# The first graph attention with joined routing: normalising and masking on ScalarE, rows rated two periods behind

## The reference

```python
h = jnp.einsum('bnf,fd->bnd', x, W)
s_src, s_dst = h @ a[:d], h @ a[d:]
e = s_src[:, :, None] + s_dst[:, None, :]
e = jnp.where(e >= 0, e, NEG_SLOPE * e)
e = jnp.where(A <= 0, -jnp.inf, e)
y = jnp.einsum('bij,bjd->bid', jax.nn.softmax(e, axis=-1), h)
...
logits = xt @ Wr + br
probs = jax.nn.softmax(logits, axis=-1)
top_p, top_idx = jax.lax.top_k(probs, TOP_K)
```

## Time and profile before

| | |
|---|---|
| time, median of 3 runs | 4688.07 us (4686.57 to 4688.72) |
| span of the profiled execution | 4591.2 us |
| what lies around the span (difference to the median) | 96.9 us |
| busy in the span: TensorE, VectorE, ScalarE, GpSimd | 76%, 62%, 46%, 39% |
| the stage in the span: first statistics, last scatter | 2700.1 us, 3049.6 us |
| end of `out(15)`, the last of the attention | 2985.9 us |

### The profile page before, as it was taken

One profiled execution on the slowest core, in us unless ns is written; L12 is line 12 of the kernel. 1 busy time (PEld: TensorE's weight loads), 2 busy tenths in 40 slices (PEclk: granted clock), 3 DMA queues, 4 the chain that ended last, 5 costly groups with the idle time before them and its releaser, 6 DMA issues. The chain is left out here.

```text
span 4591.2 us, 80959 instructions
## 1 busy us (share of the span) xinstructions
PE 3499.2 (76%) x23827; PEld 2132.6 (46%) x23827; DVE 2854.1 (62%) x10855; ACT 2105.7 (46%) x5250; POOL 1802.9 (39%) x2183
## 2 busy tenths in 40 slices
PE   3999995666666638999987867639947788884994
PEld 1333333444444423333345656627736555553663
DVE  5666656555555567777758977832247677763444
ACT  1777773322222216777753236624426555551321
POOL 3555520000000015555456225855545525544444
PEclk8999995555555559999998988869969999996997
DMA  4334318600000014333300012225442000002445
GB/s 130 112 112 118 118 53 368 261 0 0 0 0 0 0 54 126 112 112 111 89 6 2 1 57 71 70 83 153 148 156 80 32 1 20 20 20 85 129 130 162
DMA packets 237349, 378.44 MB, mean 82 GB/s; under 512 B 24832, under 2 KB 157056, under 8 KB 228672
## 3 DMA queue, kind: packets, MB, share of 16 engines
q1 hardware_dynamic: 218688, 337.44, 23.3%
q0 software_dynamic: 18432, 38.31, 2.4%
HBM read 210.70 MB, written 164.95 MB: 82 GB/s over the span
## 5 line engine op out<-in xcount | busy, mean ns | idle before, releaser
L1461 DVE CUSTOM_DVE_ANT_0 mha_seen<-mha_score,mha_mask 128x512 f32<-128x512 f32 x1024 | 684.7, 688 | 378.9 <-PE mha_score L1216 372.9
L1360 ACT ACTIVATE mha_prob<-mha_turned 128x512 f32<-128x512 f32 x1024 | 589.6, 603 | 303.1 <-PE mha_turned L1230 295.9
L1617 PE MATMUL lstm_gates<-lstm_h_part,lstm_w_part 128*128 128x16 f16 x4608 | 277.6, 179 | 327.8 <-DVE lstm_h_part L1832 324.5
L3131 POOL DMA_INDIRECT expert_rows<-expert_y,expert_target x320 | 306.9, 959 | 359.5 <-DVE expert_y L3277 154.6
L1216 PE MATMUL mha_score<-mha_k_rows,mha_q_rows 96*128 96x512 bf16 x1024 | 397.9, 391 | 56.4 <-DMA mha_k_rows<-split_rows 29.5
L1617 PEld LDWEIGHTS lstm_gates<-lstm_h_part,lstm_w_part 128*128 128x128 f16 x4608 | 217.2, 107 | 480.2 <-DVE lstm_h_part L1832 475.5
L1230 PE MATMUL mha_turned<-mha_q_rows,mha_k_rows 99*128 99x512 bf16 x1024 | 389.9, 382 | 8.4 <-ACT mha_turned L1341 6.7
L1564 POOL TENSOR_TENSOR core_mid<-lstm_hist,lstm_per_unit 128x128 f32 x64 | 29.5, 461 | 886.7 <-DVE lstm_hist L1833 886.7
L1704 ACT ACTIVATE lstm_act<-lstm_gates 128x48 f32<-128x48 f32 x512 | 108.0, 211 | 428.6 <-PE lstm_gates L1617 428.6
L1229 PE MATMUL mha_turned<-mha_maskT,core_ident_bf 128*128 128x512 bf16 x768 | 294.8, 384 | 0.3
L3169 PEld LDWEIGHTS expert_out_ps<-expert_w,expert_hid 128*128 128x128 f32 (+1 forms) x2240 | 262.4, 191 | 38.7 <-issue 33.0
(11 more groups left out here) (553 smaller groups left out, 8960.9 us busy)
## 6 DMA issues: line engine op xcount, KB each, us to landing
routed_rows<-lstm_blank SPq DMA_DIRECT2D x66, 1056.0 KB, 27.0
core_params<-adj SPq DMA_DIRECT2D x32, 1024.0 KB, 5.9
gat_adj_raw<-adj SPq DMA_DIRECT2D x32, 1024.0 KB, 5.5
mha_q_rows<-split_rows SPq DMA_DIRECT2D x64, 384.0 KB, 5.3
mha_k_rows<-split_rows SPq DMA_DIRECT2D x64, 384.0 KB, 6.0
expert_x<-routed_rows SPq DMA_DIRECT2D x80, 264.0 KB, 2.8
expert_w<-weights SPq DMA_DIRECT2D x80, 256.0 KB, 3.6
combine_pair<-expert_rows SPq DMA_DIRECT2D x32, 512.0 KB, 4.9
```

The costliest lines, as they stand in the source:

```text
L1360: act.activation(prob[:, n % RING, :], turned[n % 3][:, :], ACT.Exp, scale=-1.0).then_inc(S["prob_ready"], 1)
L1461: dve.tensor_tensor_reduce(seen[n % 2][:, :], score[n % 2][:, :], mask[1 - s][:, t, :], 1.0, 3e38, ALU.add, ALU.min, low[g][:, t, j:j + 1] ...
L1617: return pe.matmul(out, w[:, g * P:(g + 1) * P], h_part[:, part, :], start=False, stop=stop, skip_group_check=True)
L3131: pool.indirect_dma_start(out=core.y_rows[NUMBER][:, :], out_offset=bass.IndirectOffsetOnAxis(ap=target[q][:, t:t + 1], axis=0), in_=y_buf ...
```

## The change

In the first call of `gat_stage`, `normalise` moves from GpSimd to ScalarE (four activations per graph, with scale and shift as operands). `forbid` moves from VectorE to ScalarE, in two halves per graph: relu(1e30 − 1e30·adj), which is 1e30 where there is no edge; VectorE subtracts it in `masked` where it added −1e30. Rows are rated two iterations behind the attention instead of three; TensorE turns rated rows at the end of the iteration before, VectorE marks in even iterations from 4 on and picks in odd ones, behind `out`. GpSimd scatters from iteration 4 on, and the loop runs to B + 3. The logits' `take` stands behind the leaks.

```diff
-        LAST = B + 4 if route else B - 1
+        LAST = B + 3 if route else B - 1
+        MASKS = 2 if route else 1
+        forbidden = m.sb("forbidden", [P, 1]) if route else None
...
             for b in range(LAST + 1):
-                if b + 2 < B:
+                if not route and b + 2 < B:
                     normalise(b + 2)
...
-                if route and b >= 5:
-                    half = (b + 1) % 2 * T
-                    router.scatter(pool, (b - 5) // 2, range(half, half + T))
+                if route and b >= 4:
+                    half = b % 2 * T
+                    router.scatter(pool, (b - 4) // 2, range(half, half + T))
...
+            def normalise(b):
+                need(act, "xt_done", b - 1)
+                for t in range(T):
+                    last = act.activation(xn[b % 2][:, t, :], core.x_res[:, b, t, :], ACT.Identity, bias=shift[:, b, t:t + 1],
+                                          scale=rstd[:, b, t:t + 1])
+                last.then_inc(S["xn_ready"], 1)
+
+            def forbid(b, half):
+                s = b % 2
+                need(act, f"adj_in{s}", 16 * (b // 2 + 1))
+                need(act, "masked", T * (b - 1))
+                act.activation(mask[s][:, 2 * half:2 * half + 2, :], adj_raw[s][:, 2 * half:2 * half + 2, :], ACT.Relu,
+                               bias=forbidden[:, :], scale=-BIG).then_inc(S["mask_ready"], 1)
...
+            if route:
+                need(act, "stat_done", STATS[False])
+                normalise(0)
+                normalise(1)
+                need(act, "const_set", 1)
+                forbid(0, 0)
+                forbid(0, 1)
             rows_in(0)
             project(0)
             for t in range(T):
                 lower(0, t)
             exponent(0, 0)
+            if route:
+                forbid(1, 0)
+                forbid(1, 1)
             rows_in(1)
             project(1)
...
                     exponent(b, 1)
                     take(b, 0)
+                if route and 0 <= b - 2 < B:
+                    router.take_turned(act, b - 2, row_ps)
+                if inside:
                     exponent(b, 2)
                     take(b, 1)
+                if route and b + 2 < B:
+                    normalise(b + 2)
...
-                if route and 0 <= b - 2 < B:
-                    router.take_turned(act, b - 2, row_ps)
                 if inside:
                     take(b, 2)
                 if ahead:
                     lower(b + 1, 2)
-                if route and 4 <= b < B + 4 and b % 2 == 0:
-                    router.exponents(act, b // 2 - 2)
+                if route and 0 <= b - 1 < B:
+                    router.normal(act, b - 1)
                 if b + 2 < B:
                     rows_in(b + 2)
...
+                if route and b + 2 < B:
+                    forbid(b + 2, 0)
                 if b + 2 < B:
                     project(b + 2)
-                if route and 0 <= b - 1 < B:
-                    router.normal(act, b - 1)
+                if route and 3 <= b < B + 3 and b % 2:
+                    router.exponents(act, (b - 3) // 2)
+                if route and b + 2 < B:
+                    forbid(b + 2, 1)
```

More of the change, by code:

```diff
@@ L2860, in _ @@
                     back(b, 1)
[L2861 to L2864, removed]
+                if route and 4 <= b and b % 2 == 0:
+                    route_count((b - 4) // 2)
                 if b < B:
@@ L2878, in _ @@
                     project(b + 2)
+                if route and 0 <= b - 1 < B:
+                    route_turn(b - 1)
         @block.scalar
@@ L2973, in forbid @@
                 need(dve, "masked", T * (b - 1))
[L2974 to L2975 removed]
+                dve.tensor_scalar(mask[s][:, :, :], adj_raw[s][:, :, :], 0.0, -BIG, ALU.is_equal, ALU.mult).then_inc(S["mask_ready"], 1)
             def masked(b):
                 need(dve, "t_done", b + 1)
[L2979 removed]
+                need(dve, "mask_ready", MASKS * (b + 1))
                 need(dve, "turned", T * (b - 1))
                 for t in range(T):
[L2982 to L2983 removed]
+                    dve.tensor_tensor_reduce(z[b % 2][:, t, :], t_ps[:, :], mask[b % 2][:, t, :], 1.0, -3e38,
+                                             ALU.subtract if route else ALU.add, ALU.max, tmax[:, t:t + 1]).then_inc(S["masked"], 1)
             def maximum(b):
@@ L3017, in out @@
                 ins.then_inc(S["stat_out"], 1)
-            forbid(0)
-            forbid(1)
+            if not route:
+                forbid(0)
+                forbid(1)
             masked(0)
@@ L3029, in _ @@
                     maximum(b + 1)
-                if route and 5 <= b and b % 2:
-                    router.mark_rows(dve, (b - 5) // 2, t_ps)
-                if route and 0 <= b - 3 < B:
-                    router.take(dve, b - 3, rate_ps[(b - 3) % 2])
-                    if b % 2 == 0:
-                        router.lower_logits(dve, b // 2 - 2)
+                if route and 4 <= b and b % 2 == 0:
+                    router.mark_rows(dve, (b - 4) // 2, t_ps)
                 if b + 1 < B:
@@ L3038, in _ @@
                         leak(b + 1, t)
-                if b + 2 < B:
+                if route and 0 <= b - 2 < B:
+                    router.take(dve, b - 2, rate_ps[(b - 2) % 2])
+                    if b % 2:
+                        router.lower_logits(dve, (b - 3) // 2)
+                if not route and b + 2 < B:
                     forbid(b + 2)
@@ L3042, in _ @@
                     out(b)
-                if route and 4 <= b < B + 4 and b % 2 == 0:
-                    router.pick(dve, b // 2 - 2)
+                if route and 3 <= b < B + 3 and b % 2:
+                    router.pick(dve, (b - 3) // 2)
             if route:
```

23 lines of the change are left out of this document (9 added, 14 removed).

## The result

The changed kernel takes 4714.99 us in the median of 4 runs (4713.29 to 4721.51), the kernel before 4687.32 (4683.34 to 4688.72, 4 runs): ratio 1.0073, 95% interval 1.005 to 1.0097, +27.7 us. Forecast were 4688.4 us and a range from 4670 to 4705.

The account below looks back on a forecast made before the run. It took three engines as close together: ScalarE bounding short iterations, VectorE long ones, GpSimd's backlog the end. Terms +5.1 + 4.8 − 1.0 − 8.6 = +0.3 took 4688.1 to 4688.4 us, range 4670 to 4705.

Parts of the forecast that it names:

- Some 97 us around the span: Whole program: median 4688.07 less the profile's span of 4591.2, taken as lying outside the span and left unchanged.
- The pair: Graph stage, iterations 4 to 13: a short and a long iteration together 35.5 us against 35.7, five giving −1.0.
- The short iteration: Graph stage, the iteration of a pair where ScalarE sets the pace: 15.9 us forecast, against 13.90 before.
- the long one: Graph stage, the iteration of a pair where VectorE sets the pace and marks: 19.6 us forecast, against 19.80.
- `normal` fills the place of the mask: VectorE's chain in the long iteration: 1.55 us of `normal` comes in, the mask's 1.2 goes; leaks and `out` 8.5.
- The start: Graph stage before iteration 1: mask halves and `normalise` on ScalarE, less VectorE's mask, make it 5.1 us longer.
- Iterations 1 to 3: Graph stage's first iterations after iteration 0: 14.8, 15.3 and 16.3 us, together 46.4 against 41.6, +4.8.
- the mask's half: ScalarE's mask activation, 128x1024: like a copy of 1.04 us, 0.95 after overlap; one half hidden in a wait, one paid.
- The end: Graph stage from iteration 14: GpSimd arrives without backlog, so 81 us against 89.60, −8.6.
- The contention: VectorE stalled under GpSimd's `normalise`: some 1.5 us per graph goes, given no gain in the short iteration beyond 0.85.
- A new wait: Rival, slower: ScalarE's `normal(b-1)` waits for GpSimd's `scales`; 4 us later makes each pair 2 longer, 4698; chance 0.06.
- The clock rival: Rival, slower: TensorE's granted clock drops, ten iterations lose 1.3 us each on average, 4701; chance 0.19.

Follow-up runs that it names:

- before_again: The kernel before, unchanged, profiled once more: 4676.59 us against 4679.14, ratio 0.9996, span 4670.1.
- after_third: The changed kernel, unchanged, run again on a chip that holds no signals: 4605.44 us against 4594.03 for the kernel before, ratio 1.0023.
- norm_only: The kernel before with only the normalising moved from GpSimd to ScalarE, mask and router's places as before: 4691.11 us, ratio 1.003.
- after_late: The changed kernel with the graph stage's 128 scatters all behind the last iteration: iterations 4 to 13 took 186.8 us.

## Why the prediction was wrong

- **"Some 97 us around the span. I leave both as they are."** This is the step that failed at the greatest cost. Profiles since have 1.7 to 1.9 us around the span, so some 95 us lay inside the timed executions. `before_again` shows 79 of them, all in the stretches with indirect DMAs and late signals. All terms were taken from a trace without the thing that the change makes worse: with it, the middle grew by 34 us in the changed kernel and by 10 in before. Why the change makes it worse is not shown; the mask on ScalarE alone is enough for it.
- **The pair, 35.5 forecast.** 37.4 on a chip that holds nothing, 44.1 to 44.8 on one that does. The short iteration was forecast at 15.9 and is 16.0, its ScalarE 14.7 busy. The failed term is the long one. Pick (4.7) and masking with marking (6.3 for 6.4) came as forecast. But the rest from the mark's end on, put at 8.5 for leaks and `out`, took 10.5: "`normal` fills the place of the mask" left out that ScalarE and TensorE come to it late, behind the count and then at the lower clock. The iteration was mis-sized by 1.9 (21.5 for 19.6). Against the earlier trace rows the ten iterations took +8.2 instead of −1.0.
- **The start.** Forecast +5.1, measured +3.8 (from the issue of the first adjacency load to `out(0)`: 39.5 in before, 43.3 in `after_third`). Iterations 1 to 3: 49.0, not 46.4, against 41.60; the mask's half takes 1.142 us, not 1.04, which is 0.6 of the 2.6; where the rest goes was not tried. The Trainium skill's page "ScalarE: Activation LUTs", under "What ACT_TABLE_LOAD costs", has the formula that gave the estimate of 1.13 us. The trace agrees with it: its least, median and longest are 1134, 1142 and 1172 ns.
- **The end.** 82.8 against 81 forecast and 89.60 before: −6.8 for −8.6, right.
- **Sum without held signals:** +3.8 + 7.4 + 8.2 − 6.8 = +12.6, measured +11.4 (4605.44 less 4594.03). Held signals take it to +27.7 and +33. The middle alone grows by 34 in the changed kernel and by 10 in before, 24 more. What they cost elsewhere varies from chip to chip and run to run, so the sum of the windows (+41 for the stage, between two chips) and the times needn't meet.
- **The contention** was read too large, though it was given no term. The 1.67 us of the earlier trace rows is one operation of 14; the median of its line is 0.16. From iteration 1 on, before has 15 VectorE operations more than 0.3 us above their line's median, 12.6 us in all, so under 1 us a graph and not 1.5. `norm_only` and the changed kernel have none, so the stall did go with `normalise`; no time came back that can be seen.
- **The rivals.** A new wait of `normal` for the scales in the middle did not come. The clock rival looked at the short iterations, and there the clock was 1.00; the loss came in the marking one, at 0.76. No rival was a wait for a signal already due.

## What to carry over

Before summing, hold the profiled execution's own span against the timed runs: here the 2% between them was no overhead but a different condition of the chip, and one more profile of the unchanged kernel showed it. When an operation moves to another engine, ask for its side effects too: here 1.2 us of VectorE work that looked like pure load also stretched one in eight of GpSimd's scatters. And where a queue's head waits for a late result, look what behind it is ready: the count's place, together with that of `normal`, cost 3 us in the first marking iteration.

## What the hardware showed unexpectedly

- On three of the five chips of these experiments, signals of TensorE come up to 4.6 us (in the table's stretch) behind matmuls whose records had ended; in the graph stage only while GpSimd scatters or up to 2.8 us after the start of its last scatter; on the chips of `after_late` and `after_third` none does. The kernel before takes 4678.94, 4679.14 and 4700.61 us on the three and 4590.72 and 4594.03 on the two, 85 to 110 us less.
- Traces with late signals hold 37,034 to 37,920 records of signals, those without 46,425 to 46,532. Nearly all that are missing are completions of DMAs (15,805 records in the changed kernel's first trace, 24,314 in `after_third`), in the stretches with indirect DMAs. The DMA packets themselves are recorded in both alike (237,362), with the same median times. So part of the signals goes unrecorded in the stretches where others are held. Whether recording them is what holds them stays open.
